# Adding the feed forward's residual rows on TensorE, copying them out on ScalarE, and normalising the first batch of the last stage three row tiles early

## What is computed

```python
x = x + tanh(g_xattn[0]) * scan0(ctx, layernorm(x))        # y * silu(layernorm(x))
x = x + tanh(g_ffn[0])   * moe(layernorm(x))
x = x + tanh(g_xattn[1]) * scan1(ctx, layernorm(x))
x = x + tanh(g_ffn[1])   * lora_ffn(layernorm(x))

def lora_ffn(x):
    result = x @ base_w.T + base_b
    probs  = softmax(x @ router_w.T + router_b)            # 8 experts
    gate   = top-2 of probs, divided by their sum
    mid    = (x @ lora_A) * gate                           # 8 experts x rank 16
    return result + 2.0 * mid @ lora_B
```

## Time and profile before

| | |
|---|---|
| median of 3 runs | 1538.27 us (1537.59 to 1541.06) |
| the profiled execution | 1536.87 us, of which 1535.1 us are the span of the trace |
| busy share of the span | DVE 92%, PE 83%, ACT 54%, POOL 52% |
| tail, 1400 to 1536 us | PE 120 us, DVE 106 us, ACT 50 us, POOL 60 us busy |

### The profile page before, as it was taken

The page is one execution under the profiler, slowest core; times in us unless marked ns, Lnnn a source line. Parts: engine busy times, 40 slices in busy tenths (PEclk is TensorE's granted clock), DMA queues, the critical chain, the costliest instruction groups (busy, mean ns, idle before and its releaser), DMA issues.

```text
span 1535.1 us, 14497 instructions
## 1 busy us (share of the span) xinstructions
PE 1270.7 (83%) x4518; PEld 721.5 (47%) x4518; DVE 1406.7 (92%) x1462; ACT 834.5 (54%) x1341; POOL 793.1 (52%) x413
## 2 busy tenths in 40 slices
PE   6786787799699867986889998899988889926998
PEld 3322232343244324442556666666665666615555
DVE  5899999999999999998899999999899999977894
ACT  5755657564765455634865765546655444423442
POOL 0465456545544553460475456655566666565642
PEclk9898899999989998998999999999999999967999
DMA  7344445535543543360366678776786798854531
GB/s 255 99 137 125 115 130 142 141 111 143 139 138 94 142 134 100 97 172 21 93 177 232 233 247 290 228 265 233 243 275 232 268 268 269 267 163 143 167 107 56
DMA packets 99836, 264.30 MB, mean 172 GB/s; under 512 B 10832, under 2 KB 11344, under 8 KB 93616
## 3 DMA queue, kind: packets, MB, share of 16 engines
q1 hardware_dynamic: 87936, 225.36, 49.3%
q0 software_dynamic: 11440, 37.50, 7.3%
q10 hardware_dynamic: 384, 0.52, 0.1%
HBM read 233.73 MB, written 29.62 MB: 172 GB/s over the span
## 4 chain that ended last, share of the span: by engine, by line
DVE 45%; PE 18%; issue 10%; DMA 6%; POOL 5%; ACT 2%; DVEq 1%; SPq 0%; ACTq 0%; POOLq 0%
DVE state L1643 19%; DVE banks L1635 13%; PE banks L1121 6%; DMA ys_d<-expert_out 3%; DMA expert_w<-in_moe_w 3%; PE banks L1132 3%; DVE y_scan L1654 2%; POOL state L450 2%; PE banks L1285 2%; PE banks L1031 1%; PE banks L1088 1%; DVE hidden L1661 1%; DVE du L1359 1%; DVE small L1413 1%; PE banks L1080 1%
## 5 line engine op out<-in xcount | busy, mean ns | idle before, releaser
L450 POOL TENSOR_TENSOR state<-state,bc_rows 128x1024 f32<-128x1024 f32 x256 | 603.6, 2358 | 641.3 <-DVE banks L1635 641.1
L1031 PE MATMUL banks<-state,ident 128*128 128x512 f32 x640 | 329.8, 646 | 115.2 <-POOL state L450 115.1
L1643 DVE TENSOR_TENSOR_SCAN state<-decay,banks 128x1024 f32<-128x1024 f32 x176 | 402.0, 2284 | 6.3 <-ACT decay L675 1.7
L1635 DVE TENSOR_TENSOR banks<-du,bc_rows 128x1024 f32<-128x1024 f32 x256 | 314.6, 1229 | 12.8 <-issue 0.5
L1121 PE MATMUL banks<-z_gate,expert_w 128*128 128x256 f32 (+1 forms) x1504 | 285.7, 348 | 6.1 <-DMA expert_w<-in_moe_w 5.6
L1121 PEld LDWEIGHTS banks<-z_gate,expert_w 128*128 128x128 f32 x1504 | 249.9, 191 | 60.4 <-issue 20.7
L675 ACT ACTIVATE decay<-delta,neg_a 128x511 f32<-128x511 f32 x352 | 230.7, 712 | 56.9 <-DVE state L1643 52.0
L1031 PEld LDWEIGHTS banks<-state,ident 128*128 128x128 f32 x640 | 118.3, 198 | 295.2 <-POOL state L450 184.4
L1643 DVE TENSOR_TENSOR_SCAN state<-expert_w,banks 128x1024 f32<-128x1024 f32 x80 | 182.9, 2286 | 8.5 <-ACT expert_w L675 5.9
L1132 PE MATMUL banks<-expert_w,hidden 128*128 128x512 f32 x316 | 155.4, 607 | 2.9 <-DVE hidden L1664 2.9
L1654 DVE TENSOR_TENSOR y_scan<-y_scan,state 128x1024 f32<-128x1024 f32 x96 | 118.4, 1234 | 3.8 <-POOL state L450 3.8
(11 more groups left out here) (305 smaller groups left out, 1612.0 us busy)
## 6 DMA issues: line engine op xcount, KB each, us to landing
bc_rows<-bc_d SPq DMA_DIRECT2D x208, 512.0 KB, 4.9
expert_w<-in_moe_w SPq DMA_DIRECT2D x48, 1536.0 KB, 9.1
ys_d<-expert_out SPq DMA_DIRECT2D x32, 512.0 KB, 10.2
ctx_t<-in_ctxT SPq DMA_DIRECT2D x8, 512.0 KB, 6.7
x_res<-in_x SPq DMA_DIRECT2D x4, 1024.0 KB, 10.7
xn_d<-y_scan SPq DMA_DIRECT2D x4, 1024.0 KB, 7.3
ys_d<-expert_out SPq DMA_DIRECT2D x15, 256.0 KB, 9.3
out_x<-x_res SPq DMA_DIRECT2D x3, 1024.0 KB, 5.6
```

What stands on the lines that cost most here:

```text
L450: nc.gpsimd.tensor_tensor(W[:, c % 4], W[:, c % 4], bcast2(BC[:, u, 1, :]), ALU.mult).then_inc(mulc_done, 1)
L1031: mm = nc.tensor.matmul(PS[:, m], ID[:, :], W[:, c % 4, m, :], start=False, stop=True, skip_group_check=True)
L1635: nc.vector.tensor_tensor(drive(s), DU[:, s % 2, 2 * h:2 * h + 2, :], bcast2(BC[:, u, 0, :]), ALU.mult).then_inc(mulb_done, 1)
L1643: nc.vector.tensor_tensor_scan(flat(W[:, c % 4]), flat(DAS[c % da_slots(s, i)]), flat(drive(s)), 0.0, ALU.mult, ALU.add).then_inc(scan_don ...
```

## The change

Two edits, both in the tail.

The first batch's step 2 is split: mean, variance, root, bias and silu of row tiles 0 to 2 are done as soon as those tiles are combined, and the gate product of VectorE is done for three tiles and then for the fourth. The 24 products that keep TensorE busy ahead of the first y transposes wait for `rows_zn` (the bias of rows 0 to 2) where they waited for the combined rows.

The LoRA feed forward's end goes to other engines. ScalarE scales the base matrix and LoRA B by tanh(g) once, ahead of pass 0. TensorE adds X's row tiles, with the bias already in them, to the banks through the identity (`rows`, four products per batch): in passes 1 to 3 behind the LoRA B product, in pass 4 between base and the transposes of the gated product. ScalarE copies the banks to X at the end of each pass. VectorE's `lora_add` goes away. The products that keep TensorE busy ahead of the row transposes fall from 14 to 6 in passes 1 to 3.

```diff
@@ -202,6 +202,8 @@
             sem("xt_done"), sem("xst_ready"), sem("gu_done"), sem("sil_ready"), sem("h_ready"))
         hg_ready, y_done, yev, dve_step = sem("hg_ready"), sem("y_done"), sem("yev"), sem("dve_step")
 
+        rows_var, rows_std, rows_zn, rows_z = sem("rows_var"), sem("rows_std"), sem("rows_zn"), sem("rows_z")
+        ffn_scaled = sem("ffn_scaled")
         combined, exp_ready, shift_ready = sem("combined"), sem("exp_ready"), sem("shift_ready")
         mid_done, midg_ready, midt_done, midt_ready, ffn_done, x_final = (
             sem("mid_done"), sem("midg_ready"), sem("midt_done"), sem("midt_ready"), sem("ffn_done"), sem("x_final"))
@@ -631,11 +633,14 @@
 
             def z_gate(f):
                 act.wait_ge(zn_ready, 2 * f + 1)
+                z_rows(f, range(QT)).then_inc(zs_ready, 1)
+
+            def z_rows(f, qs):
                 b = f % NB
-                for q in range(QT):
+                for q in qs:
                     ins = nc.scalar.activation(ZS[:, q, :], X[:, b * QT + q, :], ACT.Silu, bias=NBI[:, q:q + 1],
                                                scale=RS[:, q:q + 1])
-                ins.then_inc(zs_ready, 1)
+                return ins
 
             def norm(f, xn):
                 act.wait_ge(zn_ready, 2 * f + 2)
@@ -914,12 +919,24 @@
 
             act.wait_ge(ld_ffn1, 16 * 4)
             nc.scalar.activation(BB, BB, ACT.Copy, scale=TG[:, 3:4]).then_inc(bias_ready, 1)
+            for w in (flat(BW), LB):
+                nc.scalar.activation(w, w, ACT.Copy, scale=TG[:, 3:4]).then_inc(ffn_scaled, 1)
             for b in range(NB + 1):
                 f, l = NB + b, b - 1
                 if l >= 0:
                     act.wait_ge(shift_ready, l + 1)
                     nc.scalar.activation(SM[:, 1, 0:QT * E1], SM[:, 0, 0:QT * E1], ACT.Exp).then_inc(exp_ready, 1)
-                if b < NB:
+                if b == 0:
+
+                    act.wait_ge(rows_var, 1)
+                    nc.scalar.activation(RS[:, 0:QT - 1], RS[:, 0:QT - 1], ACT.Sqrt).then_inc(rows_std, 1)
+                    act.wait_ge(rows_zn, 1)
+                    z_rows(f, range(QT - 1)).then_inc(rows_z, 1)
+                    act.wait_ge(var_ready, 2 * f + 1)
+                    nc.scalar.activation(RS[:, QT - 1:], RS[:, QT - 1:], ACT.Sqrt).then_inc(std_ready, 1)
+                    act.wait_ge(zn_ready, 2 * f + 1)
+                    z_rows(f, (QT - 1,)).then_inc(zs_ready, 1)
+                elif b < NB:
                     rstd_root(2 * f)
                     z_gate(f)
                 if l >= 0:
@@ -936,6 +953,11 @@
                         if q >= 2:
                             norm_t(f, xnt, (q - 2,))
                     norm_t(f, xnt, (2, 3))
+                if l >= 0:
+
+                    for q in range(QT):
+                        act.wait_ge(ffn_done, QT * l + q + 1)
+                        nc.scalar.activation(X[:, l * QT + q, :], PS[:, q], ACT.Copy).then_inc(x_final, 1)
 
 
         @block.tensor
@@ -1285,21 +1307,31 @@
                     nc.tensor.matmul(PS[:, q], xnt[:, q, k * P:(k + 1) * P], BW[:, k, :], start=(k == 0),
                                      stop=(k == ET - 1))
 
+            def rows(b, q):
+
+                return nc.tensor.matmul(PS[:, q], ID[:, :], X[:, b * QT + q, :], start=False, stop=True, skip_group_check=True)
+
             for b in range(NB + 1):
                 f, l = NB + b, b - 1
                 if l >= 0:
                     if l:
                         pe.wait_ge(x_final, QT * l)
+                    else:
+                        pe.wait_ge(ffn_scaled, 2)
                     base(l, 0)
                     base(l, 1)
                     base(l, 2)
                     base(l, 3)
+                    if b == NB:
+                        pe.wait_ge(bias_added, b)
+                        for q in range(QT):
+                            rows(l, q)
                     pe.wait_ge(midg_ready, l + 1)
                     for q in range(QT):
                         mm = nc.tensor.transpose(PRE[1][:, q * P:(q + 1) * P], MID[:, q, :], ID[:, :])
                     mm.then_inc(midt_done, 1)
                 if b == 0:
-                    pe.wait_ge(combined, TOPK * (QT - 1))
+                    pe.wait_ge(rows_zn, 1)
                     stay_warm(PRE[1], 24)
                 if b < NB:
                     y_transposes(f, Y[:, b], (0, 1))
@@ -1307,10 +1339,16 @@
                 if l >= 0:
                     pe.wait_ge(midt_ready, l + 1)
                     for q in range(QT):
-                        nc.tensor.matmul(PS[:, q], MIDT[:, q * P:(q + 1) * P], LB, start=False, stop=True,
-                                         skip_group_check=True).then_inc(ffn_done, 1)
+                        mm = nc.tensor.matmul(PS[:, q], MIDT[:, q * P:(q + 1) * P], LB, start=False, stop=True,
+                                              skip_group_check=True)
+                        if b == NB:
+                            mm.then_inc(ffn_done, 1)
+                    if b < NB:
+                        pe.wait_ge(bias_added, b)
+                        for q in range(QT):
+                            rows(l, q).then_inc(ffn_done, 1)
                 if b < NB:
-                    stay_warm(PRE[1], 14)
+                    stay_warm(PRE[1], 6 if b else 14)
                     xnt = XNT1[b % 2]
                     row_transposes(f, XN1[b % 2])
                     for q in range(QT):
@@ -1421,6 +1459,10 @@
             def scan_gate(f, y, src):
                 dve.wait_ge(zs_ready, f + 1)
                 nc.vector.tensor_tensor(flat(y), src, flat(ZS[:, :, :]), ALU.mult).then_inc(yg_done, 1)
+
+            def gate_rows(b, lo, hi):
+                y = flat(Y[:, b, lo:hi])
+                return nc.vector.tensor_tensor(y, y, flat(ZS[:, lo:hi, :]), ALU.mult)
 
             def gate_halves(f):
 
@@ -1850,11 +1892,20 @@
                 return nc.vector.bn_stats(ST[:, q, :], X[:, b * QT + q, :])
 
             def variances():
-                for q in range(QT):
+                some_variances(range(QT)).then_inc(var_ready, 1)
+
+            def some_variances(qs):
+                r = RS[:, qs[0]:qs[-1] + 1]
+                for q in qs:
                     ins = nc.vector.bn_aggr(MV[:, q, :], ST[:, q, :])
                 link(ins)
-                link(nc.vector.tensor_scalar(RS[:, :], MV[:, :, 1], EPS, None, ALU.add))
-                nc.vector.reciprocal(RS[:, :], RS[:, :]).then_inc(var_ready, 1)
+                link(nc.vector.tensor_scalar(r, MV[:, qs[0]:qs[-1] + 1, 1], EPS, None, ALU.add))
+                return nc.vector.reciprocal(r, r)
+
+            def some_bias(qs):
+                rows = slice(qs[0], qs[-1] + 1)
+                return nc.vector.scalar_tensor_tensor(out=NBI[:, rows], in0=MV[:, rows, 0], scalar=-1.0, in1=RS[:, rows],
+                                                      op0=ALU.mult, op1=ALU.mult)
 
             def tail_stats(b):
                 for q in range(QT):
@@ -1902,22 +1953,18 @@
                                                   by_expert(MIDL[h][:, :, 0:E1 * RANK1]), gates, ALU.mult)
                 ins.then_inc(midg_ready, 1)
 
-            def lora_add(b):
-                dve.wait_ge(bias_added, b + 1)
-                for q in range(QT):
-                    dve.wait_ge(ffn_done, QT * b + q + 1)
-                    xr = X[:, b * QT + q, :]
-                    nc.vector.scalar_tensor_tensor(out=xr, in0=PS[:, q], scalar=TG[:, 3:4], in1=xr, op0=ALU.mult,
-                                                   op1=ALU.add).then_inc(x_final, 1)
-
             for q in range(QT):
 
                 for k in range(TOPK):
                     combine_one(0, TOPK * q + k, q, k, 1)
-                if q < QT - 1:
-                    row_stats(0, q)
-            link(row_stats(0, QT - 1))
-            variances()
+                ins = row_stats(0, q)
+                if q >= QT - 2:
+                    link(ins)
+                if q == QT - 2:
+                    some_variances(range(QT - 1)).then_inc(rows_var, 1)
+                    dve.wait_ge(rows_std, 1)
+                    some_bias(range(QT - 1)).then_inc(rows_zn, 1)
+            some_variances((QT - 1,)).then_inc(var_ready, 1)
             for b in range(NB + 1):
                 f, l = NB + b, b - 1
                 if 0 < b < NB:
@@ -1930,12 +1977,20 @@
                     tail_stats(b)
                 if l >= 0:
                     lora_shares(l)
-                if b < NB:
+                if b == 0:
+                    dve.wait_ge(std_ready, 2 * f + 1)
+                    some_bias((QT - 1,)).then_inc(zn_ready, 1)
+                    dve.wait_ge(rows_z, 1)
+                    gate_rows(b, 0, QT - 1)
+                    dve.wait_ge(zs_ready, f + 1)
+                    gate_rows(b, QT - 1, QT).then_inc(yg_done, 1)
+                elif b < NB:
                     norm_bias(2 * f)
                 if l >= 0:
```

(5 more changed lines are left out.)

## The result

The changed kernel takes 1545.77 us (median of 8 runs, 1542.17 to 1547.31), the kernel before 1540.78 in its 8 runs of the same comparison (1537.59 to 1542.39). The ratio is 1.0037, with a 95% interval of 1.0025 to 1.0049: slower by some 5.7 us by the ratio, and 5.0 by the two medians. The forecast was 1543.8, +5.5 on the 1538.27 that the first three runs had given.

A forecast was written before the change was run, and what follows sets the result against it. It took the tail's serial chain as the bound: batch 0's head, TensorE's products with GpSimd's bias in passes 1 and 2, the end. Terms -4.7 +1.4 +1.75 +1.7 +0.8 -0.35 +1.65 +3.43 -0.15 = +5.5 on 1538.27: 1543.8 us, range 1538.5 to 1548.

The forecast's parts named there:

- The steps to the first y transposes: Batch 0's head: silu and gate product done for three tiles early, so y transposes start at 1395.9, 4.0 us earlier.
- the rival in which a switch costs double: Batch 0's head: table switches cost about twice 1.28 us, so the head gains nothing; +8.8, 1547.1 us, chance 0.04.
- at full clock: Batch 0's y transposes: they follow the 24 small products within half a microsecond, at full clock, some 0.7 us more gained.
- 1.4 for the clock alone: Before batch 0's row transposes: about 3.3 us of idle TensorE lets the clock fall; loss 1.4 us, bounds 0 and 2.9.
- the forecast's 3.3: Batch 0's head: 4.7 us gained less 1.4 for the clock, so `mid_done` comes 3.3 us early.
- Pass 1: Identity products wait for GpSimd's bias, row transposes start 2.3 us late, ScalarE and TensorE then alternate faster; net +1.75 us.
- Pass 2: Same wait for GpSimd's bias, +1.7 us, and +0.8 for a clock fall while TensorE waits about 2.8 us.
- Pass 3: TensorE sets the time: identity products 3.43 less 1.8 for fewer small products, +1.65 us, with 0.35 won back.
- the end: Between last base and the transposes: four identity products all on the path, +3.43 us, and a faster last copy, -0.15.
- the rival in which VectorE is the bound: Passes 1 and 2: losing `lora_add` frees VectorE and gathers land 2.7 us sooner; -5.2, 1533.1 us, chance 0.06.
- the one in which copies hold base back: Passes 1 to 3: ScalarE's copies delay base by 1 to 2.3 us each; about 1548 us, chance 0.10.
- bias and clock do no harm: No clock fall, passes 1 and 2 at 0.3 us each; +0.5, 1538.8 us, no change; chance 0.22.

The follow-up runs named there:

- e4_bias_first: The changed kernel with GpSimd's bias adds of batches 0 and 1 ahead of the gathers, without the wait for `xacc`: 1542.29 us, ratio 1.0012 to the kernel before.
- e11_head_again: A repeat of the kernel before with only batch 0's normalisation split; one execution, base 24.77 us after batch 0's last statistics, no total time given.
- the other old head: Profile of the kernel before with only the feed forward edit, batch 0's normalisation whole: base after 27.91 us; timed 1546.98 us, ratio 1.0047.
- the head alone: The kernel before with only the split of batch 0's normalisation, no feed forward edit: 1537.08 against 1539.98 us, ratio 0.9986.
- e8_mended: The changed kernel with VectorE doing the last add, both bias adds ahead of gathers (second after `mid_done`), 28 small products in pass 0: 1541.34 us, ratio 1.0017.
- e9_one_bias_first: The kernel before plus the split, 28 small products in pass 0 and 8 later, only batch 0's bias add ahead of gathers: 1537.63 us, ratio 0.9995.
- e7_best: The kernel before plus the split, 28 small products in pass 0, 8 later, both bias adds ahead of gathers (second after `mid_done`): 1540.04 us, ratio 1.0005.

## Why the prediction was right, and where it was not

**The head.** The steps to the first y transposes came out as written: -3.94 for -4.0, a silu of 0.81, a table load of 1.28 with the silu 0.01 behind it. That settles the rival in which a switch costs double: the last switch is on the path, and no second 1.3 us stands behind its load. The rule cited for it (the Trainium skill, ScalarE: Activation LUTs, What ACT_TABLE_LOAD costs) has its 1283 ns in these rows, and its second part not.

**What the head keeps: the step that came out otherwise.** I wrote that y transposes would run "at full clock", worth 0.7, and priced what came next at 1.4 for the clock alone. The first eight did run at full clock (1.09), the second eight did not (1.94, clock 0.77 around them): TensorE stands idle for 1.1 us between the two groups of eight records. In `e4_bias_first` and `e11_head_again` they did, 1.22 after pauses of 1.11 and 0.95, and the stretch from the first y transpose to the first row transpose took 9.89 and 9.67 for 10.54; so the 0.7 is there in some executions. The other part is a term that the sum didn't have. Work moved 4 us forward came under batch 1's gathers, and the row transposes came out 2.09 longer: 1.57 of it is the wait of ScalarE's copy, about 0.4 the clock. With gathers held back the way to the LoRA A product was 1.6 to 2.4 shorter. Over the LoRA A product the clock took 1.29 more, close to the 1.4 that I had allowed. So of 4.7 gained and 1.4 given back, 3.94 and 3.38 were measured in this pair. The missing term is shown; how large the head's whole error is, is not. Against the other old head (27.91) the new one gains 2.9 of the forecast's 3.3, and the timed runs of the head alone give 2.2, with an interval that holds both 0.6 and 3.3.

**Pass 1** +1.79 for +1.75, with a wait for the bias of 1.44; the experiment that moved the bias shows the cause. **Pass 2** +0.85 for +2.5: mechanism right, size off. TensorE waited 1.61 for the bias instead of some 2.8, because GpSimd came to its bias 0.95 us sooner behind `mid_done` than in the kernel before, whose rows I had used (17.40 us from base's start to the bias for 18.35), and at 1.61 the clock stayed at 1.00, so the 0.8 for it fell away. **Pass 3** +1.44 for +1.30, **the end** +3.30 for +3.28.

**The covers.** ScalarE's four copies end 0.95 us before base starts, as counted (0.9): ScalarE, then VectorE at the gather, kernel after.

```profile
1448.94 2.06 ACT L960 ACTIVATE x_res<-banks 128x512 f32<-128x512 f32 x4
```

```profile
1448.30 0.75 DVE L1878 SCALAR_TENSOR_TENSOR x_res<-y_scan,slot_w,x_res 128x512 f32<-128x512 f32 x1 [1.70 <-DMA y_scan<-ys_d,slots]
```

Base starts at 1451.95, the copies are done at 1451.00. VectorE's wait for the gather grew from 1.08 to 1.70, so what `lora_add` freed went into waiting: the rival in which VectorE is the bound has fallen, and so has the one in which copies hold base back. The rival "bias and clock do no harm" fails on both waits for the bias and on the clock in the head.

**Two errors that cancel.** The forecast was near the measured time with two terms off by 2.7 (in this pair of executions) and 1.65 in opposite directions. That the sum agrees to within 0.5 us (+5.5 for 5.0 and 5.7) is in part luck, and it is less certain than the agreement suggests.

**What stays open.** Which resource the gathers and TensorE share is not shown; I only know that the hold-ups seen lie in the traffic, and that the one at the row transposes is gone when the gathers are held back. Nor is it shown why it can end in the middle of the traffic, as in `e8_mended`, or why it strikes harder in some executions than in others, nor what of the 1.3 us ahead of the last statistics belongs to the change.

## What to carry to other kernels

An add that another engine does in time it has to spare costs the path little or nothing (0.75 us at the end of the kernel before); given to TensorE in front of a serial end, it costs its full length (3.43 us here), and a wait for the slowest contributor comes with it. When an early stage is made quicker, look at what its successors will now run beside: here some 1.6 of the 3.9 us gained went to gathers in flight in the profiled execution. Split a change and time the parts: the half that was good (-2.2 us by the ratio, -2.9 with more small products) was hidden in a sum of +5.7. And profile a stretch more than once before its tenths are believed: the old head took 25.59 us in one execution and 27.91 in another.

## What the hardware showed that was not expected

- TensorE can slow or stop while indirect gathers land, though its operands are ready: 1.75 and 1.16 us between single small instructions at a DMA share of 0.72, none at 0.01 (`e9_one_bias_first`); the LoRA A product 1.6 to 2.4 us later than with gathers held back. The share alone isn't enough for it: from 1404 to 1408 in `e9_one_bias_first` TensorE was busy all 4.00 us at a share of 0.73. The Trainium skill (SBUF — State Buffer, Who interferes with whom) has DMA and compute engines never contending; if that holds, what is shared here lies elsewhere than in SBUF's ports, and no run here shows where.
- A GpSimd add of 128x2048 with two SBUF operands and VectorE's combines stretch each other: 6.50 for 4.55 in `e4_bias_first`, and one combine of 4.90 for 0.75 (4.88 in `e7_best`, 5.02 in `e8_mended`).
- The clock fell between short bursts of the kernel after: 1.00 from 1398 to 1399, 0.55 from 1399 to 1400, with no idle stretch near it longer than 1.11 us. In `e4_bias_first` it stood at 1.00 over the same pause of 1.11, and in the kernel with 28 small products over one of 1.05 at the row transposes. So such a pause doesn't decide it.
